# A fused attention and expert kernel on one core: the third and fourth score tile of a step wait together, and three edits in the order behind the attention

## The chip, the cores and the metric

One NeuronCore of a Trainium2 chip runs the whole program. The metric is the device time of one execution in microseconds (us). Engines are named as in the profile: PE is TensorE's matmuls, PEld its weight loads, ACT is ScalarE, DVE is VectorE, POOL is GpSimd, SP is the queue that issues most DMAs. L944 is line 944 of the kernel before.

## The reference

A text stream x (4 sequences, 512 tokens, 256 wide) attends to a context of 1601 rows, and then goes through a mixture of experts:

```python
x = x + tanh(g_xattn[0]) * xattn(layernorm(x), ctx, ...)     # 16 heads of 16
x = x + tanh(g_ffn[0])   * experts(layernorm(x), ...)        # one shared, 8 routed, top 2

def xattn(x, y):
    q, k, v = x @ Wq + bq, y @ Wk + bk, y @ Wv + bv
    out = softmax(q k^T / 4) v                                # per head
    return relu(out @ W1 + b1) @ W2 + b2
```

All is float32. In most products a float32 operand is split into a rounded part ("hi") and a rest ("lo"), both of which TensorE takes in one pass; the product is then hi·hi + lo·hi + hi·lo.

## The kernel before, in words

The attention runs in 16 units (a batch of the four, times a group of four heads). A unit has 13 steps, one for each tile of up to 128 context rows, so there are 208 steps. The engines have queues of their own, written out by hand, and semaphores between them.

A step m on PE has, in this order: two score tiles (`st`, L944: 64 contraction rows, 128 context rows by 512 tokens), a "score pair" (`score`, L929, which computes scores of the next unit of which only maxima are wanted), the other jobs of the step (Q, K, V, W1, ... in other units few or none), a second score pair, two more score tiles, and the values of the step before (`pv`, L959: four heads side by side in 32 columns each, read from `probs`). ACT turns each score tile into exponentials (`exp`, L770, which writes `probs`), DVE takes the maxima of the score pairs (L1079).

Score tiles and jobs share a ring of three PSUM banks (`ring_ps`). Whoever takes a bank waits in `free_bank` until the bank's user before it has been read. The tiles of a step are 4m-1, 4m, 4m+1 and 4m+2; in a step without jobs the third (4m+1) takes the bank of tile 4m-2, and the fourth (4m+2) that of tile 4m-1. So the fourth waits for the exponential of the first tile of its own step. Tiles of an even number use rows 0 to 63 of the array, those of an odd number rows 64 to 127 (`rows` in `st`), so each pair of a step has one of each. In the last unit the ring has five banks, two of them from `gu_ps`.

Behind the steps stand the last jobs: SUM (transposes the result), OT (transposes it back, split by ACT into `ot_hi` and by DVE into `ot_lo`), four W1 products of six matmuls each, two W2 products. Between them `begin_shared(t, f, k)` starts the shared expert for token tiles 0 and 1: half k of the contraction of gate (f=0) or up (f=1) into `gu_ps`. The last step also has the job LG (transposes of logits, L892), which reads what DVE copied from the job LT (L887, L1098). After a barrier (L370) the second part of the kernel runs; its first matmuls are `gate_up(1)` (L1463), then the transposes of tile 0's hidden values (L1472).

Of the kernel before, what the change touches and what calls it, by code (L numbers as in the profile page):

```python
# [28 lines left out]
B, N, D = 4, 512, 256  # L29
# [10 lines left out]
MT = (M + P - 1) // P  # L40
# [3 lines left out]
UNITS = B * H // 4  # L44
# [264 lines left out]
def attention(nc, I, x1, stats, mv, veps, power, rstd, tg, ident, rows_dram,  # L309
# [16 lines left out]
    def tiles_of(m):  # L326

        first, last = (2 if m > MT * (UNITS - 1) else 0), (2 if m >= MT * (UNITS - 1) else 0)
        return list(range(max(4 * m - 1 + first, 0), min(4 * m + 3 + last, 4 * MT * UNITS)))
# [40 lines left out]
    with ExitStack() as ctx:  # L370
# [418 lines left out]
        def _(pe):  # L789
# [29 lines left out]
            def do(job):  # L819
# [39 lines left out]
                elif kind == "V":  # L859
                    _, b, g = job  # L860
                    for mt in range(2 * g, min(2 * g + 2, MT)):
                        last = value_tile(slot, b, mt)
                elif kind == "MX":
                    pe.wait_ge(mx_ready, job[1] + 1)
                    last = nc.tensor.transpose(slot[0:16, 0:P], mx[:].rearrange("p h t -> p (h t)"), ident[:])
                elif kind == "SUM":
                    pe.wait_ge(pv_free, job[1] + 2)
                    for t in range(NT):
                        last = nc.tensor.transpose(slot[:, t * P:(t + 1) * P], osb[:, t * P:(t + 1) * P], ident[:])
                elif kind == "OT":  # L870
                    _, b, dt = job
                    pe.wait_ge(free_dve, freed["SUM", 4 * b + 3])
                    heads = slice(dt * P // HD, (dt + 1) * P // HD)
                    for t in range(NT):
                        last = nc.tensor.transpose(slot[:, t * P:(t + 1) * P],
                                                   onT[:, t, heads, :].rearrange("p h d -> p (h d)"), ident[:])
                elif kind == "XT2":
                    _, b, k = job
                    pe.wait_ge(xn2_ready, NT * (b + 1))
                    for t in range(NT):  # L880
                        last = nc.tensor.transpose(slot[:, t * P:(t + 1) * P],
                                                   xn2[:, b * NT + t, k * P:(k + 1) * P], ident[:])
                elif kind == "LT":
                    b = job[1]
                    pe.wait_ge(free_dve, freed["XT2", b, 1])
                    for k in range(2):
                        last = nc.tensor.matmul(slot[0:E, :], wr[:, k, :], xn2T[:, b * NT:(b + 1) * NT, k, :],  # L887
                                                start=(k == 0), stop=(k == 1))
                elif kind == "LG":
                    pe.wait_ge(free_dve, freed["LT", job[1]])  # L890
                    for t in range(NT):
                        last = nc.tensor.transpose(slot[:, t * E:(t + 1) * E], across[:, t * P:(t + 1) * P],  # L892
                                                   ident[0:E, 0:E])
                elif kind == "W1":
                    _, b, f = job
                    pe.wait_ge(w1_parted, 2 * min(b + 1, B - 1))
                    pe.wait_ge(free_dve, freed["OT", b, 1])
                    products = [(w, x) for k in range(2) for w, x in ((w1_hi[:, k], ot_hi[:, k, :]),
                                                                      (w1_lo[:, k], ot_hi[:, k, :]),
                                                                      (w1_hi[:, k], ot_lo[:, k, :]))]  # L900
                    for n, (w, x) in enumerate(products):
                        last = nc.tensor.matmul(slot, w[:, f * P:(f + 1) * P], x, start=(n == 0),
                                                stop=(n == len(products) - 1))
                elif kind == "W2":
                    _, b, half = job
                    pe.wait_ge(free_act, freed["W1", b, F1 // P - 1])
                    for i in range(2):
                        t = 2 * half + i
                        for k in range(F1 // P):
                            last = nc.tensor.matmul(slot[:, i * D:(i + 1) * D], h1[:, k, t * P:(t + 1) * P],  # L910
                                                    w2[:, k, :], start=(k == 0), stop=(k == F1 // P - 1))
# [56 lines left out]
            for item in first + early:  # L968
# [4 lines left out]
                else:  # L973
                    do(item)
            pe.wait_ge(free_dve, freed["MX", 0])
            for u, mt, chunk, jobs in steps:
                m = MT * u + mt
                lead = 2 if m > 0 else 1
                for idx in tiles_of(m)[:lead]:
                    st(idx)  # L980
                for pair in chunk[0:1]:
                    score(pair)
                for job in jobs:
                    if not ahead_of_values(u, job):
                        do(job)
                for pair in chunk[1:2]:
                    score(pair)
                for idx in tiles_of(m)[lead:]:
                    st(idx)
                for pair in chunk[2:]:  # L990
                    score(pair)
                for job in jobs:
                    if ahead_of_values(u, job):
                        do(job)
                if m > 0:
                    pv(m - 1)
            pv(MT * UNITS - 1)

            def begin_shared(t, f, k):
# [5 lines left out]

            pe.wait_ge(ws_loaded, 80)
            pe.wait_ge(free_dve, freed["XT2", 0, 1])
            waits = [("SUM", UNITS - 1), ("OT", B - 1, 0), ("W1", B - 1, 0), ("W2", B - 1, 0)]
            for job in last_jobs:
                if job in waits:  # L1010
                    n = waits.index(job)
                    begin_shared(0, n // 2, n % 2)
                do(job)
            pe.wait_ge(exp_done, 4 * MT * UNITS)
            begin_shared(1, 0, 0)

        @block.vector
        def _(dve):
# [163 lines left out]
def experts(nc, I, O, x1, stats, mv, veps, power, rstd, tg, ident, rows_dram, picked_dram, shared, lists,  # L1182
            gate_hi, up_hi, gu_ps, gu_full):
    xn2, xn2T, wgu_s, wd_s, wr, rb, logit = shared
    with ExitStack() as ctx:
# [195 lines left out]
        def _(pe):  # L1381
# [50 lines left out]
            def gate_up(i):  # L1432
# [9 lines left out]
                for f in range(2):  # L1442
# [6 lines left out]
                            pe.wait_ge(owner_ready, 1)  # L1449
                        owners[r + 1] = pe.value_load(owner[0:1, r + 1:r + 2], min_val=0, max_val=E - 1)  # L1450
                    if tile_of(i) is not None:
                        begun = i == 1 and f == 0
                        products = [(xn2T[:, tile_of(i), k, :], wgu_s[:, k, f * F2:(f + 1) * F2])
                                    for k in range(begun, 2)]
                    else:
                        e, begun = bass.ds(owners[r], 1), False
                        products = []
                        for k in range(2):
                            hi, lo = (up_hi if f else gate_hi)[:, e, k, :], wgu_lo[:, e, k, f * F2:(f + 1) * F2]
                            x_hi, x_lo = xb_hi[:, r % 2, k, :], xb_lo[:, r % 2, k, :]  # L1460
                            products += [(x_hi, hi), (x_hi, lo), (x_lo, hi)]
                    for n, (x, w) in enumerate(products):
                        last = nc.tensor.matmul(gu_ps[:, i % 2, f, :], x, w, start=(n == 0 and not begun),  # L1463
                                                stop=(n == len(products) - 1))
                last.then_inc(gu_full, 1)

# [295 lines left out]
```

## Time and profile before

| | |
|---|---|
| median of 3 runs | 1035.18 us (1034.99 to 1036.46) |
| the profiled execution | 1034.86 us |
| its span, first to last instruction | 1033.1 us |
| granted clock of TensorE | 0.998 |
| PE busy | 1011.9 us, 98% |
| DVE busy | 680.7 us, 66% |
| ACT busy | 612.1 us, 59% |

The steps of the attention lie between about 56 and 714 us of the span, the last jobs between 714 and 734 us. PE counts as busy nearly everywhere, since a matmul's record lasts until its last result is out; how close the array is to its limit must be read from the starts of the matmuls.

### The profile page before, as it was taken

How to read it: one execution, taken by the hardware profiler on the slowest of the kernel's cores; microseconds unless marked ns; L12 is line 12 of the kernel's file. 1: busy time of each engine (PE TensorE's matmuls, PEld its weight loads, DVE VectorE, ACT ScalarE, POOL GpSimd, SP SyncE). 2: the span in 40 equal slices, each digit the busy share in tenths (PEclk: the TensorE clock that was granted, in tenths of full speed). 3: DMA queues.
4: the chain of work that ended last, by engine and by line, in shares of the span. 5: the costliest groups of instructions: out<-in, count | busy, mean ns of one | idle time of the engine just before them, and what ended most of it. 6: DMA issues, size and time to landing. Idle time of an engine off the chain costs nothing. (4 is left out here: it accounts for less than half of the span.)

```text
span 1033.1 us, 15853 instructions
## 1 busy us (share of the span) xinstructions
PE 1011.9 (98%) x5821; PEld 559.6 (54%) x5821; DVE 680.7 (66%) x929; ACT 612.1 (59%) x1144; POOL 227.8 (22%) x225
## 2 busy tenths in 40 slices
PE   8899999999999999999999999998999999999998
PEld 5434445434445434544544453333666888888865
DVE  4999886896787798588788768712487322222227
ACT  3167777886677777577787767774375222222211
POOL 6129300105400103610010031020002333333310
PEclk9999999999999999999999999999999999999999
DMA  9263030430302403203033030011591111111107
GB/s 220 72 169 63 2 64 4 125 64 2 64 14 52 107 22 64 55 10 65 1 64 65 1 64 1 18 66 41 175 336 30 39 51 53 53 51 52 48 26 244
DMA packets 38282, 70.17 MB, mean 68 GB/s; under 512 B 6848, under 2 KB 23360, under 8 KB 38208
## 3 DMA queue, kind: packets, MB, share of 16 engines
q1 hardware_dynamic: 33072, 57.88, 21.6%
q0 software_dynamic: 3744, 10.23, 3.2%
q10 hardware_dynamic: 1392, 1.05, 0.4%
q8 instruction: 49, 0.80, 0.3%
q14 instruction: 25, 0.20, 0.1%
HBM read 33.70 MB, written 9.31 MB: 42 GB/s over the span
## 5 line engine op out<-in xcount | busy, mean ns | idle before, releaser
L770 ACT ACTIVATE probs<-ring_ps 128x512 f32<-128x512 f32 x816 | 434.0, 598 | 125.8 <-PE ring_ps L944 118.8
L1079 DVE TENSOR_REDUCE mpart<-gu_ps 128x2 f32<-128x1024 f32 x384 | 456.4, 1220 | 71.3 <-PE gu_ps L929 71.2
L944 PE MATMUL ring_ps<-qst,kst 64*128 64x512 f32 x816 | 221.8, 459 | 3.0 <-ACT probs L770 2.1
L959 PE MATMUL pv_ps<-probs,vp 128*32 128x512 f32 (+2 forms) x1664 | 222.7, 604 | 0.6 <-ACT osb L701 0.6
L944 PEld LDWEIGHTS ring_ps<-qst,kst 64*128 64x128 f32 x816 | 97.3, 180 | 205.4 <-ACT probs L770 116.2
L929 PE MATMUL gu_ps<-kst,qst 63*128 63x512 f32 (+1 forms) x1024 | 179.7, 396 | 8.7 <-DVE mpart L1079 7.5
L929 PEld LDWEIGHTS gu_ps<-kst,qst 63*128 63x128 f32 x1024 | 91.7, 185 | 64.1 <-DVE mpart L1079 40.3
L1309 ACT ACTIVATE h_sb<-gu_ps 128x512 f32<-128x512 f32 x55 | 32.8, 596 | 133.6 <-PE gu_ps L1463 133.6
L1516 DVE TENSOR_TENSOR h_sb<-h_sb,gu_ps 128x512 f32<-128x512 f32 x55 | 37.7, 686 | 112.6 <-ACT h_sb L1309 112.1
L1483 PE MATMUL y_ps<-wd,hT 128*128 x312 | 73.8, 379 | 0.0
L1300 POOL DMA_INDIRECT picked<-ysb,target x39 | 38.5, 988 | 131.5 <-DVE ysb L1557 131.5
L959 PEld LDWEIGHTS pv_ps<-probs,vp 128*32 128x32 f32 (+2 forms) x1664 | 32.9, 107 | 57.8 <-issue 42.4
L1463 PE MATMUL gu_ps<-wgu_lo,xb_hi 128*128 x156 | 61.2, 392 | 0.0
L304 POOL TENSOR_SCALAR veps<-mv 128x4 f32<-128x4 f32 x8 | 1.9, 233 | 266.9 <-DVE mv L1048 113.9
L1483 PEld LDWEIGHTS y_ps<-wd,hT 128*128 128x128 f32 x312 | 56.2, 190 | 6.0
L630 POOL TENSOR_SCALAR c_hi<-w 128x1024 fp32r<-128x1024 f32 x3 | 8.3, 2775 | 223.2 <-PE ring_ps L806 223.2
L1463 PE MATMUL gu_ps<-cold,parts 128*128 128x512 f32 x118 | 53.8, 597 | 0.3 <-PEq L370 0.3
L1287 POOL DMA_INDIRECT xb<-rows,token x39 | 40.7, 1044 | 56.7 <-DVE token L1635 34.8
L1315 ACT ACTIVATE xb_hi<-t_ps 128x256 fp32r<-128x256 f32 x39 | 15.0, 385 | 49.3 <-PE t_ps L1429 49.3
L1557 DVE COPY ysb<-y_ps 128x256 f32<-128x256 f32 x39 | 16.6, 425 | 33.1 <-PE y_ps L1483 33.1
L742 ACT ACTIVATE vp<-ring_ps 128x512 f32<-128x512 f32 (+1 forms) x28 | 15.9, 568 | 32.2 <-PE ring_ps L806 32.2
L1463 PEld LDWEIGHTS gu_ps<-cold,parts 128*128 128x128 f32 x118 | 22.4, 193 | 22.7 <-issue 21.9
(240 smaller groups left out, 1251.8 us busy)
## 6 DMA issues: line engine op xcount, KB each, us to landing
kst<-parts SPq DMA_DIRECT2D x45, 401.0 KB, 5.3
qst<-parts SPq DMA_DIRECT2D x48, 128.0 KB, 4.5
wgu<-in_WgT SPq DMA_DIRECT2D x16, 256.0 KB, 8.2
wgu<-in_WuT SPq DMA_DIRECT2D x16, 256.0 KB, 8.3
wd<-in_WdT SPq DMA_DIRECT2D x8, 512.0 KB, 9.8
wgu<-picked SPq DMA_DIRECT2D x8, 512.0 KB, 7.4
cold<-in_ctxT SPq DMA_DIRECT2D x3, 800.5 KB, 4.2
cold<-in_ctxT SPq DMA_DIRECT2D x6, 400.2 KB, 5.9
```

Of the source, the lines that this page charges most:

```text
L770: nc.scalar.activation(probs[0:w, m % NPB, h, :], bank_of(("st", idx))[0:w], ACT.Exp, scale=SCALE).then_inc(exp_done, 1)
L929: last = nc.tensor.matmul(out, qst[u % NKB][rows, p, i * P:(i + 1) * P], kst[u % NKB][rows, p, keys], start=True, stop=True)
L944: nc.tensor.matmul(bank_of(("st", idx))[0:w], kst[u % NKB][rows, h // 2, mt * P:mt * P + w], qst[u % NKB][rows, h // 2, :], start=True, st ...
L959: last = nc.tensor.matmul(pv_ps[32 * h:32 * h + c1 - c0, :], values[:, c0:c1], probs[0:w, m % NPB, h, :], start=(mt == 0), stop=(mt == MT ...
L1079: nc.vector.tensor_reduce(mpart[:, :, p, t, q], s_ps[:, n % NSP], AX.X, ALU.max).then_inc(s_free, 1)
L1287: pool.indirect_dma_start(xb[:, r % NXB, :], None, rows_dram[:], bass.IndirectOffsetOnAxis(ap=token[:, r:r + 1], axis=0)).then_inc(xb_load ...
L1300: pool.indirect_dma_start(picked_dram[:], bass.IndirectOffsetOnAxis(ap=target[:, r:r + 1], axis=0), ysb[:, r % NXB, :], None).then_inc(y_s ...
L1309: nc.scalar.activation(h_sb[:, i % 2, :], gu_ps[:, i % 2, 0, :], ACT.Silu).then_inc(silu_done, 1)
L1463: last = nc.tensor.matmul(gu_ps[:, i % 2, f, :], x, w, start=(n == 0 and not begun), stop=(n == len(products) - 1))
L1483: last = nc.tensor.matmul(y_of(i), hT[:, i % 2, k, :], w, start=(k == 0), stop=(k == FK - 1))
L1516: nc.vector.tensor_tensor(h_sb[:, i % 2, :], h_sb[:, i % 2, :], gu_ps[:, i % 2, 1, :], ALU.mult).then_inc(h_ready, 1)
L1557: nc.vector.tensor_copy(ysb[:, r % NXB, :], y_ps[:, 0:D]).then_inc(y_out, 1)
```

## The change

- In the steps of all units but the last, PE waits for the banks of the third and the fourth tile before it issues the third.
- The last step's LG moves from ahead of the values of step 206 to behind them.
- W1: the four products with `ot_hi` go first and wait for ACT's part alone; the wait for DVE's `ot_lo` stands before the fifth.
- `begin_shared`: the second half of the up product goes ahead of W1 with the first, half a gate of tile 1 goes ahead of W2, and the other half stands at the end. The second part's `gate_up(1)` then has no gate matmuls.

```diff
@@ W1 in do(job)
-                    pe.wait_ge(free_dve, freed["OT", b, 1])
-                    products = [(w, x) for k in range(2) for w, x in ((w1_hi[:, k], ot_hi[:, k, :]),
-                                                                      (w1_lo[:, k], ot_hi[:, k, :]),
-                                                                      (w1_hi[:, k], ot_lo[:, k, :]))]
+                    pe.wait_ge(hi_ready, hi_count["OT", b, 1])
+                    products = ([(w[:, k], ot_hi[:, k, :]) for k in range(2) for w in (w1_hi, w1_lo)] +
+                                [(w1_hi[:, k], ot_lo[:, k, :]) for k in range(2)])
                     for n, (w, x) in enumerate(products):
+                        if n == 4:
+                            pe.wait_ge(free_dve, freed["OT", b, 1])
@@ the steps
+            last_logits = steps[-1][3][-1]
...
+                if u < UNITS - 1:
+                    for idx in tiles_of(m)[lead:]:
+                        free_bank(bank_owner(("st", idx)))
                 for idx in tiles_of(m)[lead:]:
                     st(idx)
...
-                    if ahead_of_values(u, job):
+                    if ahead_of_values(u, job) and job != last_logits:
                         do(job)
                 if m > 0:
                     pv(m - 1)
+            do(last_logits)
             pv(MT * UNITS - 1)
@@ behind the steps
-            waits = [("SUM", UNITS - 1), ("OT", B - 1, 0), ("W1", B - 1, 0), ("W2", B - 1, 0)]
+            pe.wait_ge(exp_done, 4 * MT * UNITS)
             for job in last_jobs:
-                if job in waits:
-                    n = waits.index(job)
-                    begin_shared(0, n // 2, n % 2)
+                if job == ("SUM", UNITS - 1):
+                    begin_shared(0, 0, 0)
+                elif job == ("OT", B - 1, 0):
+                    begin_shared(0, 0, 1)
+                elif job == ("W1", B - 1, 0):
+                    begin_shared(0, 1, 0)
+                    begin_shared(0, 1, 1)
+                elif job == ("W2", B - 1, 0):
+                    begin_shared(1, 0, 0)
                 do(job)
-            pe.wait_ge(exp_done, 4 * MT * UNITS)
-            begin_shared(1, 0, 0)
+            begin_shared(1, 0, 1)
@@ gate_up(i) of the second part
-                                    for k in range(begun, 2)]
+                                    for k in range(2) if (i, f) != (1, 0)]
```

PE's queue in a step whose third tile takes the bank of a job, before: two tiles, two score pairs, the third tile, the fourth tile, the values.

```order
L944 MATMUL ring_ps<-qst0,kst0 128x512 [waits exp_done] x2
L929 MATMUL gu_ps<-kst2,qst2 128x512 [waits s_free]
L929 MATMUL gu_ps<-kst2,qst2 128x512
L929 MATMUL gu_ps<-kst2,qst2 128x512 [waits s_free]
L929 MATMUL gu_ps<-kst2,qst2 128x512
L944 MATMUL ring_ps<-qst0,kst0 128x512 [waits free_dve]
L944 MATMUL ring_ps<-qst0,kst0 128x512 [waits exp_done]
L959 MATMUL pv_ps<-probs,vp 32x512 [waits exp_done]
```

The same place of the changed kernel, from the second score pair on.

```order
L930 MATMUL gu_ps<-kst2,qst2 128x512 [waits s_free]
L930 MATMUL gu_ps<-kst2,qst2 128x512
L945 MATMUL ring_ps<-qst0,kst0 128x512 [waits free_dve,exp_done]
L945 MATMUL ring_ps<-qst0,kst0 128x512 [waits exp_done]
L960 MATMUL pv_ps<-probs,vp 32x512 [waits exp_done]
```

The matmuls stand where they stood; the wait of the fourth tile now stands ahead of the third as well. In a step without jobs both waits are for `exp_done`, so that the row reads as before ("[waits exp_done] x2"), but there too a semaphore instruction with both counts has come in front. PE's queue has 366 semaphore instructions before and 561 after: 195 more, one for each step of 15 units.

PE's queue at the end of the steps and behind it, before: LT, LG, values of step 206, values of step 207, then the last jobs up to the first W1.

```order
L887 MATMUL gu_ps<-parts,wr 8x512
L892 MATMUL ring_ps<-ident,across 128x8 [waits free_dve]
L892 MATMUL ring_ps<-ident,across 128x8 x3
L959 MATMUL pv_ps<-probs,vp 32x512 [waits exp_done]
L959 MATMUL pv_ps<-probs,vp 32x512 x2
L959 MATMUL pv_ps<-probs,vp 17x512
L959 MATMUL pv_ps<-probs,vp 32x512 [waits exp_done]
```

The same place after.

```order
L887 MATMUL gu_ps<-parts,wr 8x512
L960 MATMUL pv_ps<-probs,vp 32x512 [waits exp_done]
L960 MATMUL pv_ps<-probs,vp 32x512 x2
L960 MATMUL pv_ps<-probs,vp 17x512
L892 MATMUL ring_ps<-ident,across 128x8 [waits free_dve]
L892 MATMUL ring_ps<-ident,across 128x8 x3
L960 MATMUL pv_ps<-probs,vp 32x512 [waits exp_done]
```

LG has moved behind the values of step 206 and ahead of those of step 207. The third place is the first W1 of the last jobs; after the change PE has there:

```order
L1007 MATMUL gu_ps<-cold,parts 128x512 x2
L903 MATMUL ring_ps<-ot_hi,c0_hi 128x512 [waits hi_ready,w1_parted,free_dve]
L903 MATMUL ring_ps<-ot_hi,c1_both 128x512
L903 MATMUL ring_ps<-ot_hi,c0_hi 128x512
L903 MATMUL ring_ps<-ot_hi,c1_both 128x512
L903 MATMUL ring_ps<-xt_hi,c0_hi 128x512 [waits free_dve]
```

Before, one `begin_shared` matmul (L1001) stood there instead of two, and W1's first matmul waited for `free_dve` and `w1_parted`. (`xt_hi` is the memory of `ot_lo`, `c0_hi` and `c1_both` that of W1's parts.)

## Rows read from the trace of the kernel before

**Rows 1.** The page: engine totals, and the group of exponentials.

```profile
PE 1011.9 (98%) x5821; PEld 559.6 (54%) x5821; DVE 680.7 (66%) x929; ACT 612.1 (59%) x1144; POOL 227.8 (22%) x225
...
L770 ACT ACTIVATE probs<-ring_ps 128x512 f32<-128x512 f32 x816 | 434.0, 598 | 125.8 <-PE ring_ps L944 118.8
```

**Rows 2.** Busy time (PE, PEld, DVE, ACT, POOL) in a unit without jobs.

```profile
181.00:214.00 33.00, 33.00 (x220) 13.20 (x216) 28.72 (x30) 26.20 (x52) 3.71 (x2) 1.00 0.36 98
```

**Rows 3.** Timeline of one step without jobs: start, length, [idle before <-releaser].

```profile
210.31 0.18 PEld L944 LDWEIGHTS ring_ps<-qst,kst 64*128 64x128 f32 x2 [0.84 <-ACT probs L770]
210.84 2.07 ACT L770 ACTIVATE probs<-ring_ps 128x512 f32<-128x512 f32 x4 [0.80 <-PE ring_ps L944]
211.11 0.88 PE L944 MATMUL ring_ps<-qst,kst 64*128 64x512 f32 x2
211.49 0.18 PEld L944 LDWEIGHTS ring_ps<-qst,kst 64*128 64x128 f32 x1 [0.40 <-ACT probs L770]
211.92 1.06 PE L959 MATMUL pv_ps<-probs,vp 128*32 128x512 f32 x8
212.90 0.18 PEld L944 LDWEIGHTS ring_ps<-qst,kst 64*128 64x128 f32 x2 [0.84 <-ACT probs L770]
```

**Rows 4.** Waits of PEld (us, times, longest) in 60:93, 181:214, 215:256, 307:350, 639:672.

```profile
PEld ring_ps L944 <- ACT probs L770: 10.2, 15, 0.8
...
PEld ring_ps L944 <- ACT probs L770: 12.3, 20, 0.8
...
PEld ring_ps L944 <- ACT probs L770: 6.0, 9, 0.8
...
PEld ring_ps L944 <- ACT probs L770: 2.1, 3, 0.8
...
PEld ring_ps L944 <- ACT probs L770: 14.0, 21, 0.9
```

**Rows 5.** Timeline at SUM and OT, whose waits stand in semaphore instructions.

```profile
714.28 0.60 ACT L701 ACTIVATE osb<-pv_ps 128x512 f32<-128x512 f32 x1 [3.65 <-PE pv_ps L959]
715.00 0.14 PEld L869 LDWEIGHTS ring_ps<-ident,osb 128*128 128x128 f32 x1 [0.56 <-issue]
...
716.03 0.42 DVE L1144 TENSOR_TENSOR onT<-ring_ps,rden 128x256 f32<-128x256 f32 x1
716.57 0.14 PEld L875 LDWEIGHTS ring_ps<-ident,onT 128*128 128x128 f32 x1 [0.84 <-issue]
```

**Rows 6.** Timeline of a step with a V job: third and fourth tile, values.

```profile
158.71 0.40 PE L944 MATMUL ring_ps<-qst,kst 64*128 64x512 f32 x2
...
159.04 1.07 PE L959 MATMUL pv_ps<-probs,vp 128*32 128x512 f32 x8
```

**Rows 7.** Timeline of the last step: LT, its copy, LG, values.

```profile
709.23 1.88 PE L887 MATMUL gu_ps<-parts,wr 128*8 128x512 f32 x4 [0.18 <-ACT probs L770]
...
711.15 0.68 DVE L1098 COPY across<-gu_ps 8x512 f32<-8x512 f32 x1 [2.96 <-PE gu_ps L887]
...
711.98 0.38 PE L892 MATMUL ring_ps<-ident,across 8*128 8x8 f32 x4 [0.86 <-DVE across L1098]
...
712.29 1.92 PE L959 MATMUL pv_ps<-probs,vp 128*32 128x512 f32 x16
```

**Rows 8.** Timeline at the first W1 of the last jobs.

```profile
717.50 1.02 PE L1001 MATMUL gu_ps<-cold,parts 128*128 128x512 f32 x2
...
718.78 0.74 DVE L1115 SCALAR_TENSOR_TENSOR xt_hi<-ring_ps,bv,ot_hi 128x512 fp32r<-128x512 f32 x1
...
719.67 0.47 PE L902 MATMUL ring_ps<-ot_hi,c_hi 128*128 128x512 f32 x1 [1.15 <-DVE xt_hi L1115]
```

**Rows 9.** Timeline at the start of the second part.

```profile
734.69 2.81 PE L1463 MATMUL gu_ps<-cold,parts 128*128 128x512 f32 x6 [0.30 <-PEq L370]
...
736.58 0.69 DVE L1516 TENSOR_TENSOR h_sb<-h_sb,gu_ps 128x512 f32<-128x512 f32 x1
...
737.32 0.42 PEld L1472 LDWEIGHTS ht_ps<-ident,h_sb 128*128 128x128 f32 x4 [0.64 <-DVE h_sb L1516]
```

More of the change, by code:

```diff
@@ L1451, in gate_up @@
                     if tile_of(i) is not None:
-                        begun = i == 1 and f == 0
                         products = [(xn2T[:, tile_of(i), k, :], wgu_s[:, k, f * F2:(f + 1) * F2])
-                                    for k in range(begun, 2)]
+                                    for k in range(2) if (i, f) != (1, 0)]
                     else:
-                        e, begun = bass.ds(owners[r], 1), False
+                        e = bass.ds(owners[r], 1)
                         products = []
@@ L1462, in gate_up @@
                     for n, (x, w) in enumerate(products):
-                        last = nc.tensor.matmul(gu_ps[:, i % 2, f, :], x, w, start=(n == 0 and not begun),
+                        last = nc.tensor.matmul(gu_ps[:, i % 2, f, :], x, w, start=(n == 0),
                                                 stop=(n == len(products) - 1))
```

## The prediction

> **What bounds the kernel now.** I read the page first: PE is busy 98% of the span, ACT 59%, DVE 66% [rows 1]. That does not tell which of them a step waits for, so I went to the stretches and then to one step. A unit without jobs (181 to 214 us) has 13 steps in about 34 us, and DVE is busy 28.7 of 33 us and ACT 26.2 [rows 2]: neither is full. The timeline of one step shows why it takes 2.59 us all the same (210.31 to 212.90) [rows 3]. The reader is to follow one chain through it: the first pair of tiles starts at 210.31; its first exponential at 210.84, and it lasts 0.60 [rows 1], to 211.44; the fourth tile, whose bank that exponential frees, loads at 211.49, after an idle 0.40 that ACT ended; the values follow at 211.92, and the next step's first pair at 212.90. 0.53 + 0.60 + 0.05 + 0.43 + 0.98 = 2.59: the chain is closed, with no slack in it, and it runs through the wait of the fourth tile.
>
> How often is that so? The waits of the weight loads of L944 for ACT mix two kinds: the pair behind the values, 0.84 each (the values themselves lie in that time), and the fourth tile, 0.40 to 0.43. In 181 to 214 us there are 20 with 12.3 us: 9 of 0.84 and 11 of 0.43. In the same way 60 to 93 us has 6 of the short kind, 639 to 672 us has 9, 215 to 256 us has 4, and 307 to 350 us, a unit with many jobs, has 1 [rows 4]. The units repeat this by batch. Three units are like the first of these (11 each), units 13 and 14 have 9 each, unit 0 has 6, three units 4 each, six units 1 or 2: 33 + 18 + 6 + 12 + 9 = 78. Some of these waits are put down to the values or to another engine in the views, so I take 85 of the 195 changed steps as steps in which the fourth tile's wait closes the chain.
>
> **The joint wait.** It takes no matmul away. What it can do is start the third tile later, or change how PE waits.
>
> The third tile: in the step shown it started at 211.11, ran with nothing behind it, and the fourth came at 211.49 (the two records together 0.88) [rows 3]. They use different rows of the array, and the values stand behind the fourth. So delaying the third by 0.4 frees nothing, and nothing on PE is later for it. On ACT the third tile's exponential comes later: it followed the first two at 211.82 (four of them take 2.07 and one 0.60, so they start 0.49 apart) [rows 1, 3], and now needs the tile, 0.53 behind its start. With the tile at 211.56 it starts at 212.09 and ends at 212.69; its bank is wanted at 212.90. It is covered by 0.2 us. Without that cover it costs what it is late, up to 0.3 us a step; I put 0.5 us for the few steps with less room (ends of units, job steps).
>
> How PE waits: before, the fourth tile's own load carried the wait, and it started 0.05 us after the exponential's end (211.44 to 211.49) [rows 3]. Now the last wait to end stands in a semaphore instruction. The trace shows what that costs where it is already so: the exponential's place is taken by ACT's copy, which ends at 714.88, and SUM's load starts at 715.00, after 0.11 to 0.12; DVE's product ends at 716.45 and OT's load starts at 716.57, the same again [rows 5]. So the wait takes 0.115 instead of 0.05, 0.065 us more, on a chain without slack. In 85 steps that is 5.5 us. Below, it is nothing (if the engine hides it); above, it is 195 x 0.065 = 12.7 us (if every step passes it on). I take 5.5, since in the job steps the tiles come long after the exponentials and the matmuls of the jobs cover the instruction.
>
> The Trainium skill (Perfetto Trace Analysis, Identifying Dependency Chains) says that an instruction that waits for several engines may have semaphore instructions put in front of it; it gives no price. The rows above are the price, and the trace agrees that they stand there.
>
> **LG behind the values.** Before, PE stood from the end of LT until DVE's copy ended at 711.83, started LG at 711.98 and the values of 206 at 712.29, those of 207 one half of 1.92, some 0.88, later, at 713.17 [rows 7]. LT's fourth matmul record ends at 711.11; values can follow there at about 711.05 (0.07 before the end of the last record, as at 211.92 in [rows 3], where the tile before ran to 211.99). They take 0.98 until other work may start (211.92 to 212.90 [rows 3]), so LG starts at 712.03 and is past DVE's copy, and the values of 207 start 0.31 later, at 712.34. Gain: 0.83 us. If LG waited once more, the gain would be smaller, not below 0.
>
> **W1 and the begun products.** W1's first matmul stood at 719.67, 0.15 behind DVE's `ot_lo` (718.78 + 0.74 = 719.52). The begun product ahead of it started at 717.50 and has two records of 0.43 each, so four end at 719.22 [rows 8]. ACT's `ot_hi` is done before that. W1 starts at about 719.25: gain 0.42 us. Its fifth matmul comes 0.9 later and finds `ot_lo` done. The half gate ahead of W2 takes the place of the half up there, and the last one that of the one before: 0. W1 in the other three batches stands a step or more behind OT, so its new wait is long over: 0.
>
> In the second part `gate_up(1)` has four matmul records instead of six, 0.86 us less on PE. But the transposes behind it waited for DVE: 736.58 + 0.69 = 737.27, and their load starts at 737.32 [rows 9]. DVE's work there starts at the barrier and does not change. So 0; if the transposes had followed PE alone, 0.86.
>
> **Sum**, against the profiled execution: 1034.86 + 5.5 + 0.5 - 0.83 - 0.42 = 1039.6; it lies 0.3 below the median of the runs, so I say 1040.0 us. A difference under 0.2%, 2.1 us, is about what a measurement of this kernel cannot tell from no change.
>
> **Rivals.** (A) The semaphore instruction costs nothing in the steps, or DVE absorbs it: DVE is busy 28.7 of 33 us [rows 2], and a score pair that waits for it takes up what PE is late. For it: in units with jobs this must happen. Against it: in the step shown PE's wait for the fourth tile comes after both score pairs. Only the last jobs' 1.25 us remain, and the time is 1034.0 us.
>
> (B) Two tiles that start together leave the array sooner. In the job step the pair was together at 158.71 and the values came 0.33 later [rows 6]; behind the lone fourth tile they came 0.43 later [rows 3]. If the joint start earns that 0.10, it pays 0.10 - 0.065 = 0.035 in 85 steps, 3.0 us: 1034.9 + 0.3 - 3.0 - 1.25 = 1030.9 us. It decides as soon as it earns more than the 0.065 in these steps. Against it: at 158.71 the two had their weights loaded ahead, since nothing was waited for (records of 0.40 against 0.49), and a joint wait leaves both loads behind the wait. The Trainium skill (TensorE: Matmul & The Clock Gate, Part 3) has matmuls in different row groups run at once, which would speak for such a gain. The trace agrees on the overlap, but the chain here does not stand on the array's time.
>
> (C) The two counts in one semaphore instruction cost twice: 0.13 in 85 steps, 11 us, 1045 us. I see no row for it.
>
> **Numbers.** My forecast (1037.3 to 1042.5 alone) 0.62, A 0.19, B 0.14, C 0.05. Of A, most lies within 0.2% (1033.1 to 1037.3), a small part below it; a tenth of my own case, with half of the steps absorbed, lies there as well. Slower 0.62, same 0.22, faster 0.16. The range from 1032.0 to 1043.0 leaves out most of B and C.
>
> **What the profile will show.** In a step without jobs, third and fourth tile start together, 0.12 behind the first exponential's end, and the step takes 2.65 instead of 2.59 us; the unit from 181 us is 0.8 longer; units with many jobs are as long as before. The values of 206 start ahead of LG, W1 starts 1.75 behind the first begun product, and the last jobs, from the values of 207 to the barrier, are 0.4 shorter. PE is idle about 0.9 ahead of the second part's first transposes. I am wrong if the load of the third tile starts 0.05 behind the exponential, or if the values then come 0.33 behind the pair.

## The result and the profile after

The changed kernel takes 1039.7 us, the median of 6 runs (1038.48 to 1040.11), against 1035.17 us of the kernel before (6 runs, 1034.94 to 1036.46). The ratio is 1.0041, with a 95% interval of 1.0029 to 1.0054: it is slower, and the forecast of 1040.0 us is met. The profiled execution took 1039.84 us with a span of 1038.1 us, 5.0 us more than the span before, at a granted clock of 1.0. Below it turns out that two of the forecast's terms were off and that a third, of which it knew nothing, made up for them by luck.

The page, engine totals and exponentials (as in [rows 1]):

```profile
PE 1000.1 (96%) x5821; PEld 547.0 (53%) x5821; DVE 680.9 (66%) x929; ACT 621.6 (60%) x1144; POOL 230.1 (22%) x225
...
L770 ACT ACTIVATE probs<-ring_ps 128x512 f32<-128x512 f32 x816 | 442.5, 595 | 122.1 <-PE ring_ps L945 104.0
```

PE's busy time has gone down by 11.8 us while the kernel became slower: the records of two matmuls that start together lie over each other, and that time counts once. The number says nothing about the work; the starts do.

The timeline of one step without jobs, as in [rows 3] (L945 is now the score tile, L960 the values):

```profile
211.70 0.19 PEld L945 LDWEIGHTS ring_ps<-qst,kst 64*128 64x128 f32 x2 [0.84 <-ACT probs L770]
...
212.23 1.09 ACT L770 ACTIVATE probs<-ring_ps 128x512 f32<-128x512 f32 x2 [0.58 <-PE ring_ps L945]
...
212.90 0.22 PEld L945 LDWEIGHTS ring_ps<-qst,kst 64*128 64x128 f32 x2 [0.60 <-DVE mneg L1147]
212.93 0.50 PE L945 MATMUL ring_ps<-qst,kst 64*128 64x512 f32 x2 [0.25 <-issue]
213.36 0.15 PEld L960 LDWEIGHTS pv_ps<-probs,vp 128*32 128x32 f32 x8 [0.25 <-ACT probs L770]
...
214.35 0.18 PEld L945 LDWEIGHTS ring_ps<-qst,kst 64*128 64x128 f32 x2 [0.84 <-ACT probs L770]
```

The step takes 214.35 - 211.70 = 2.65 us, where it took 2.59. The first exponential ends 0.60 after 212.23, at 212.83; the third tile's load follows at 212.90, 0.07 behind it, and the fourth's 0.03 behind that. (The view names DVE as the releaser of 212.90, since the third tile of this step takes a bank that DVE has read, but it is ACT's exponential that ended just before.) The fourth tile's matmul stands 0.10 behind the exponential instead of 0.05, and the values again 0.42 behind it. The whole chain is the old one with some 0.05 us put in at one place.

The waits of PEld in 182 to 215 us, as in [rows 4]: there were 20 with 12.3 us, and the ones of the fourth tile are now of the third, which waits longer.

```profile
PEld ring_ps L945 <- ACT probs L770: 14.0, 21, 0.8
PEld pv_ps L960 <- ACT probs L770: 2.4, 10, 0.2
PEld gu_ps L930 <- DVE mpart L1090: 1.9, 7, 0.3
```

The last step, as in [rows 7]. The values of step 206 now follow LT at 715.42, LG stands at 716.85 and the values of 207 at 717.16:

```profile
715.42 1.42 PE L960 MATMUL pv_ps<-probs,vp 128*32 128x512 f32 x5
...
716.02 0.68 DVE L1109 COPY across<-gu_ps 8x512 f32<-8x512 f32 x1 [2.96 <-PE gu_ps L887]
...
716.85 0.38 PE L892 MATMUL ring_ps<-ident,across 8*128 8x8 f32 x4
...
717.16 1.06 PE L960 MATMUL pv_ps<-probs,vp 65*32 65x512 f32 x8
```

LG still starts 0.15 behind the end of DVE's copy (716.70), and no longer holds anything up: the values of 206 fill that time.

The first W1 of the last jobs, as in [rows 8], and the start of the second part, as in [rows 9]:

```profile
721.51 1.88 PE L1007 MATMUL gu_ps<-cold,parts 128*128 128x512 f32 x4
...
722.12 1.41 DVE L1126 SCALAR_TENSOR_TENSOR xt_hi<-ring_ps,bv,ot_hi 128x512 fp32r<-128x512 f32 x2 [1.66 <-ACT ot_hi L749]
...
722.83 0.80 PE L903 MATMUL ring_ps<-ot_hi,c_hi 128*128 128x512 f32 x1
...
738.22 1.96 PE L1473 MATMUL gu_ps<-cold,parts 128*128 128x512 f32 x4 [0.30 <-PEq L370]
...
740.10 0.69 DVE L1526 TENSOR_TENSOR h_sb<-h_sb,gu_ps 128x512 f32<-128x512 f32 x1
...
740.84 0.42 PEld L1482 LDWEIGHTS ht_ps<-ident,h_sb 128*128 128x128 f32 x4 [1.50 <-DVE h_sb L1526]
```

PEld idles 1.50 us ahead of the transposes, 0.86 more than before: the two matmuls that the second part no longer has are turned into idle time.

Where the 5.0 us of span went, by the starts of the same work in both traces:

| stretch | before | after | change |
|---|---|---|---|
| start of the last LT matmul | 710.52 | 715.39 | +4.87 |
| from there to the first begun product | 3.62 | 2.76 | -0.86 |
| from there to the first W2 of the last jobs | 12.25 | 11.76 | -0.49 |
| from there to the second part's first transposes | 10.95 | 10.93 | -0.02 |
| from there to the last output transfer's issue | 293.69 | 293.71 | +0.02 |
| from its issue to its landing | 1.69 | 3.15 | +1.46 |

The last line was in nobody's sum. Between 1034.5 and 1037.5 us the DMA view of the kernel after has the lines below: one packet on q8, which moves code, and one output transfer that takes 3.1 us to land. The kernel before has no line of q8 in its last 4 us, and its last two transfers have a median of 1.7 us.

```profile
q8 instruction: 1, 0.02, 3.0%
issues: line engine op xcount, KB each, median us to landing
out<-x SPq DMA_DIRECT2D x1, 128.0 KB, 3.1
```

### The profile page after: what moved, and what is told of

The parts are those of the page before. It is cut to its first block and busy times, and to the rows that moved or that the text cites. A ratio compares the mean times of both kernels' runs of the same rounds, so it can differ in the third digit from the quotient of the medians.

```text
span 1038.1 us, 16048 instructions
## 1 busy us (share of the span) xinstructions
PE 1000.1 (96%) x5821; PEld 547.0 (53%) x5821; DVE 680.9 (66%) x929; ACT 621.6 (60%) x1144; POOL 230.1 (22%) x225
## 5 line engine op out<-in xcount | busy, mean ns | idle before, releaser
L770 ACT ACTIVATE probs<-ring_ps 128x512 f32<-128x512 f32 x816 | 442.5, 595 | 122.1 <-PE ring_ps L945 104.0
L960 PE MATMUL pv_ps<-probs,vp 128*32 128x512 f32 (+2 forms) x1664 | 223.7, 604 | 0.6 <-ACT osb L701 0.6
L945 PE MATMUL ring_ps<-qst,kst 64*128 64x512 f32 x816 | 198.5, 469 | 18.0 <-ACT probs L770 14.7
L945 PEld LDWEIGHTS ring_ps<-qst,kst 64*128 64x128 f32 x816 | 80.2, 180 | 224.4 <-ACT probs L770 135.4
L930 PE MATMUL gu_ps<-kst,qst 63*128 63x512 f32 (+1 forms) x1024 | 177.1, 396 | 8.2 <-DVE mpart L1090 6.4
L960 PEld LDWEIGHTS pv_ps<-probs,vp 128*32 128x32 f32 (+2 forms) x1664 | 33.1, 107 | 57.3 <-issue 32.8
L1298 POOL DMA_INDIRECT xb<-rows,token x39 | 42.9, 1101 | 54.1 <-DVE token L1645 34.8
L1482 PEld LDWEIGHTS ht_ps<-ident,h_sb 128*128 128x128 f32 x220 | 27.2, 141 | 15.1 <-issue 5.8
```

What stands on the lines that cost most here:

```text
L770: nc.scalar.activation(probs[0:w, m % NPB, h, :], bank_of(("st", idx))[0:w], ACT.Exp, scale=SCALE).then_inc(exp_done, 1)
L930: last = nc.tensor.matmul(out, qst[u % NKB][rows, p, i * P:(i + 1) * P], kst[u % NKB][rows, p, keys], start=True, stop=True)
L945: nc.tensor.matmul(bank_of(("st", idx))[0:w], kst[u % NKB][rows, h // 2, mt * P:mt * P + w], qst[u % NKB][rows, h // 2, :], start=True, st ...
L960: last = nc.tensor.matmul(pv_ps[32 * h:32 * h + c1 - c0, :], values[:, c0:c1], probs[0:w, m % NPB, h, :], start=(mt == 0), stop=(mt == MT ...
L1298: pool.indirect_dma_start(xb[:, r % NXB, :], None, rows_dram[:], bass.IndirectOffsetOnAxis(ap=token[:, r:r + 1], axis=0)).then_inc(xb_load ...
L1482: last = nc.tensor.transpose(ht_ps[:, i % 2, k * P:(k + 1) * P], h_sb[:, i % 2, k * P:(k + 1) * P], ident[:])
```

## The experiments

Each kernel was run beside the kernel before, whose medians were 1035.09 us beside the first four, 1035.22 beside the next four and 1035.27 beside the last two. Ratios are to the kernel before, with their 95% intervals. "Closed steps" are the 124 of the 195 changed steps in which, in the trace of before, the fourth tile's load starts within 0.06 us of an exponential's end.

**What the joint wait and the other three edits do apart.** The changed kernel without the joint wait, which leaves the steps as they were:

```diff
-                if u < UNITS - 1:
-                    for idx in tiles_of(m)[lead:]:
-                        free_bank(bank_owner(("st", idx)))
                 for idx in tiles_of(m)[lead:]:
                     st(idx)
```

> The changed kernel without the joint wait: LG behind the values, W1 and the begun products alone. Its trace showed 0.86 us gained at LG and 0.49 us at W1, and 0 in the second part. If these are independent of the steps, the kernel is 1.35 us faster than before, 1033.8 us, and the steps take as long as before. Rival: the last output's transfer, which took 3.15 us in the changed kernel against 1.69 before, is slow because of the tail edits; then 1035.3 us, and the last transfer again takes about 3.1 us.

And the kernel before with those three lines put in and nothing else:

> The kernel before with the joint wait alone. The steps lose the 4.9 us that the changed kernel's trace shows up to the last step: 1040.1 us. If the slow last transfer (1.46 us) comes from the 195 added instructions through a code fetch that falls on it, the exact place of the fetch decides: up to 1041.5 us with it. Rival: the loss needs the other edits too; then below 1039 us.

Without the joint wait: 1033.87 us (11 runs), ratio 0.9992 (0.9982 to 1.0001). With it alone: 1040.01 us (5 runs), ratio 1.0046 (1.0032 to 1.0059). The two expectations hold: the whole loss is the joint wait's, and the other edits bring some 1.2 us that it buries. Its step, in the timeline of the kernel with the joint wait alone:

```profile
211.34 0.50 PE L944 MATMUL ring_ps<-qst,kst 64*128 64x512 f32 x2
...
212.54 0.22 PEld L944 LDWEIGHTS ring_ps<-qst,kst 64*128 64x128 f32 x2 [0.60 <-DVE mneg L1139]
...
213.99 0.50 PE L944 MATMUL ring_ps<-qst,kst 64*128 64x512 f32 x2
```

It is the step of the kernel after, 2.65 us.

**Is it the common start or the semaphore instruction?** Both edits here are made to the changed kernel without the joint wait. In the first both tiles start together, but the third tile's own matmul carries the later count and the fourth asks for nothing, so there is no semaphore instruction (where a job held one of the banks, the tiles wait as before):

```diff
@@ st
-                free_bank(bank_owner(("st", idx)))
+                if bank_freed_by is None:
+                    free_bank(bank_owner(("st", idx)))
+                elif bank_freed_by[0] == "later":
+                    pe.wait_ge(exp_done, bank_freed_by[1])
@@ the steps
-                for idx in tiles_of(m)[lead:]:
-                    st(idx)
+                rest = tiles_of(m)[lead:]
+                holders = [bank_owner(("st", idx)) for idx in rest]
+                if u < UNITS - 1 and len(rest) == 2 and all(h is not None and h[0] == "st" for h in holders):
+                    st(rest[0], ("later", max(h[1] for h in holders) + 1))
+                    st(rest[1], ("held",))
+                else:
+                    for idx in rest:
+                        st(idx)
```

> The tail edits, and a joint start without a semaphore instruction: where both banks were held by score tiles, the third tile's own load waits for the later exponential and the fourth's has no wait; where a job held one of them, the tiles wait as before. Theory from the changed kernel's trace (third load 0.069 behind the exponential, fourth 0.101, against 0.051 for the fourth before): 0.032 of the 0.050 lost per step is the second load of the pair being issued behind the wait, so here the fourth load comes 0.083 behind, 88 steps lose 0.032 each, 2.8 us, and the kernel takes 1036.6 us. Rival: all the loss is the semaphore instruction; the fourth load comes 0.054 behind, nothing is lost, 1033.9 us. Second rival, a pair that starts together clears the array sooner: below 1033 us.

In the second the tiles start as before, apart, and the fourth tile alone has its wait in a semaphore instruction:

```diff
-                for idx in tiles_of(m)[lead:]:
+                for n, idx in enumerate(tiles_of(m)[lead:]):
+                    if n == 1 and u < UNITS - 1:
+                        free_bank(bank_owner(("st", idx)))
                     st(idx)
```

> The tail edits, and in the same 195 steps a semaphore instruction with the fourth tile's wait ahead of the fourth alone; the third starts early, as before. Theory: the semaphore instruction itself costs 0.018 (0.069 against 0.051), so 88 steps lose 1.6 us: 1035.4 us, and up to 1.5 more if the code fetch falls on the last transfer. Rival of my prediction: the instruction costs 0.065 as at SUM and OT, 5.7 us: 1039.5 us. Rival: it costs the whole 0.050 and the pair's common start nothing: 1038.2 us.

The first took 1035.04 us (11 runs, ratio 1.0002, 0.9993 to 1.0011), with loads 0.051 and 0.054 us behind the exponential: the 0.03 us between the two loads, which I had put down to the common start, are not there without the instruction. The other took 1041.25 us (5 runs, ratio 1.0056, 1.0043 to 1.007), with the fourth tile's load 0.113 behind. Both expectations had the size wrong, in opposite directions, and together they say that the semaphore instruction is the cause of nearly all of the loss: the common start without it costs the closed steps 0.35 us in all. (The first kernel's median is 1.17 us above that of the kernel without the joint wait, 1033.87; its runs lie at 1034.07 to 1035.38 and four of them at 1036.72 to 1037.09, and its trace shows no more than the 0.35.) A step of the kernel with the instruction ahead of the fourth tile:

```profile
213.01 1.58 ACT L770 ACTIVATE probs<-ring_ps 128x512 f32<-128x512 f32 x3 [0.81 <-PE ring_ps L945]
213.07 0.18 PEld L945 LDWEIGHTS ring_ps<-qst,kst 64*128 64x128 f32 x1
...
213.72 0.18 PEld L945 LDWEIGHTS ring_ps<-qst,kst 64*128 64x128 f32 x1 [0.46 <-ACT probs L770]
```

The exponential ends at 213.61 and the load stands at 213.72; before it was 0.05 behind. (Its profiled execution, 1043.13 us, also lost 1.36 us once in the last unit, where the edit does nothing.)

**Does an instruction cost anything whose count is there already?** Where several counts are asked for, the matmul carries the one asked for first and the instruction the others. So the order of two waits decides which of them stands in the instruction. In the changed kernel the later count does, beside the older one that the matmul carries too; here the order is turned round:

```diff
-                    for idx in tiles_of(m)[lead:]:
+                    for idx in reversed(tiles_of(m)[lead:]):
                         free_bank(bank_owner(("st", idx)))
```

> The changed kernel with the two early waits asked in the other order (fourth tile's bank first). There are as many semaphore instructions as in the changed kernel, but the instruction now holds only the count of the third tile's bank, which has long been reached, and the third tile's matmul itself carries the later count, of the first exponential. Theory (only the wait that ends last costs something when it stands in a semaphore instruction): the loads of the third and the fourth tile come 0.05 us behind the exponential as in the tail-only kernel, steps of 2.60 us, time 1034.0 to 1034.5, or 1035.5 if the code transfer falls on the last output transfer again (1.45 us). Rival (every semaphore instruction costs PE's queue its time, wherever the wait is): as slow as the changed kernel, 1038.3 to 1039.7.

And 195 instructions that never wait, ahead of the values, on top of the last jobs' edits:

```diff
                 pe.wait_ge(exp_done, 4 * (m + 1))
+                if u < UNITS - 1:
+                    pe.wait_ge(pool_ready, 2)
```

> The tail edits alone, plus a semaphore instruction ahead of each step's values in 15 units (195 of them), whose count (POOL's at the start of the kernel) has been reached since the start. Theory (an instruction whose count is there costs the steps nothing, since the values' own wait, 0.4 us behind the fourth tile, covers it; what it does is lengthen the program, so that a 16 KB piece of code is fetched on top of the last output transfer): steps 2.60 us, last transfer 3.1 instead of 1.7 us, 1035.3. Rival 1 (each costs 0.02 to 0.06 on the closed chain, between the fourth tile and the values): 1036 to 1041. Rival 2 (the long last transfer of the changed kernel and of the fourth-tile kernel has another cause than the program's length): 1033.9.

1034.83 us (11 runs, ratio 0.9993, 0.9984 to 1.0002) and 1034.59 us (11 runs, ratio 0.9994, 0.9985 to 1.0004). Both have the 561 semaphore instructions of the changed kernel and hardly any of its loss. The 124 closed steps together are longer by 0.38 and 0.13 us, against 4.61 in the changed kernel. The step of the kernel with the order turned round, with a common start and 2.60 us:

```profile
210.64 0.50 PE L945 MATMUL ring_ps<-qst,kst 64*128 64x512 f32 x2
211.18 2.26 ACT L770 ACTIVATE probs<-ring_ps 128x512 f32<-128x512 f32 x4 [0.60 <-PE ring_ps L945]
211.82 0.19 PEld L945 LDWEIGHTS ring_ps<-qst,kst 64*128 64x128 f32 x2 [0.58 <-ACT probs L770]
...
213.24 0.49 PE L945 MATMUL ring_ps<-qst,kst 64*128 64x512 f32 x2
```

The exponential ends at 211.77 or 211.78, and the pair's loads stand at 211.82, 0.05 behind. The waits that the traces record in this step agree: here the third tile's load waits for ACT's count and the instruction for DVE's alone, while in the changed kernel the load waits for DVE's and the instruction for both. The theory holds, and its rival (each instruction costs its time) falls. The part of it on the program's length falls too: here the last transfer took 1.7 us.

**Why 0.05 a step in one case and 0.065 in the other?** First the number of counts, with two in the instruction ahead of the fourth tile:

```diff
                     if n == 1 and u < UNITS - 1:
                         free_bank(bank_owner(("st", idx)))
+                        free_bank(bank_owner(("st", idx - 1)))
```

> As the kernel with a semaphore instruction ahead of the fourth tile alone (1041.3 us, load 0.113 us behind the exponential, step +0.065), but the instruction holds two counts, the fourth tile's and the third's, as it does in the changed kernel. Theory (how late the load is depends on where the instruction stands and not on how many counts it holds): the fourth tile's load again 0.113 behind the exponential, 1041.3 less up to 0.5. Rival (an instruction with two counts is quicker after the last of them): load at 0.07, steps +0.02 to +0.03, 1037 to 1038.

It took 1040.29 us (5 runs, ratio 1.0049, 1.0036 to 1.0063), with the load again 0.113 behind the exponential and the closed steps longer by 6.13 us, as with one count (6.20). Not the number, then. Next what the matmul behind the instruction carries. In the changed kernel it is an old count, ahead of the fourth tile it was the fresh one. So once the changed kernel with the fresh count on the third tile's matmul, and once the other with the old one on the fourth's:

```diff
@@ the changed kernel
-                    for idx in tiles_of(m)[lead:]:
+                    for idx in 2 * tiles_of(m)[-1:]:
                         free_bank(bank_owner(("st", idx)))
@@ the instruction ahead of the fourth tile
-                        free_bank(bank_owner(("st", idx)))
+                        free_bank(bank_owner(("st", idx - 1)))
```

> The changed kernel with other counts in the same places: the semaphore instruction ahead of the third tile still holds both counts, but the third tile's own matmul now also carries the later one, which has only just been reached. In the changed kernel the matmul behind the instruction carries the older count and its load comes 0.069 us behind the exponential (steps +0.050); where the instruction stands ahead of the fourth tile its matmul carries the same count as the instruction, and the load comes 0.113 behind (steps +0.065). Theory (it is this second look at the same fresh count that makes the one dearer than the other): the third tile's load comes 0.11 behind here, the fourth's 0.03 later, and the steps lose 0.06 to 0.09, time 1041 to 1043. Rival (the place in the queue makes it): loads at 0.069 and 0.101 as in the changed kernel, 1038.5 to 1039.7.

> As the kernel with a semaphore instruction ahead of the fourth tile alone (load 0.113 us behind the exponential, steps +0.065, 1041.3 us), but the fourth tile's matmul now carries the third tile's older count and the instruction alone holds the fourth's. Theory of the second look: load at 0.069, steps +0.02, about 1036. Rival (the place in the queue makes it): load at 0.113, steps +0.065, 1040 to 1041.

1038.24 us (5 runs, ratio 1.0034, 1.0021 to 1.0047), loads at 0.069 and 0.101; and 1039.89 us (6 runs, ratio 1.0052, 1.0038 to 1.0067), load at 0.114. Both stayed as their place in the queue had them, so the theory behind these two runs (a second look at the same fresh count makes the load later) fell twice. The timeline of the second:

```profile
212.44 2.06 ACT L770 ACTIVATE probs<-ring_ps 128x512 f32<-128x512 f32 x4 [0.80 <-PE ring_ps L945]
212.50 0.18 PEld L945 LDWEIGHTS ring_ps<-qst,kst 64*128 64x128 f32 x1
...
213.15 0.18 PEld L945 LDWEIGHTS ring_ps<-qst,kst 64*128 64x128 f32 x1 [0.47 <-issue]
```

The traces also record the semaphore instructions themselves, and there the two places differ. First the one of the changed kernel's step at 212.9, then the one of the kernel with the instruction ahead of the fourth tile, at 213.7 (the three numbers are the shortest, median and longest record, in ns):

```profile
L798 PEldq EVENT_SEMAPHORE  x1: 589/589/589, 212.3 to 212.3; - x1
...
L794 PEldq EVENT_SEMAPHORE  x1: 51/51/51, 213.6 to 213.6; - x1
```

In the changed kernel, in the one with the joint wait alone and in the one with the fresh count on the third tile's matmul, the record begins 0.13 us or more ahead of the exponential's end in all 124 closed steps, ends 0.041 to 0.045 behind it, and the load starts 0.024 to 0.027 after that. In the three kernels with the instruction ahead of the fourth tile the record begins only 0.036 to 0.038 behind the exponential's end, lasts 0.051 (as does that of an instruction whose count is there already), and the load again starts 0.024 to 0.026 later. The instructions at SUM and OT in the kernel before, from which the forecast took its price, are of this second kind: 0.051 long, beginning about 0.04 behind the end of ACT's copy and of DVE's product. So it is dearer where the record begins only when the count comes. Why it begins no earlier there (the last matmul ahead of it is a lone third tile, and a score pair in the changed kernel) stays open.

The kernel with the fresh count on the third tile's matmul is also a second sample of the changed kernel: its steps are the same, its last transfer takes 1.7 us, and its median is 1.5 us lower. Its runs lie at 1037.95 to 1038.24 (three) and at 1039.63 and 1039.83, so the medians alone would be weak evidence.

**LG alone.** The kernel before with `do(last_logits)` behind the loop:

```diff
+            last_logits = steps[-1][3][-1]
...
-                    if ahead_of_values(u, job):
+                    if ahead_of_values(u, job) and job != last_logits:
                         do(job)
                 if m > 0:
                     pv(m - 1)
+            do(last_logits)
```

> The kernel before with LG moved behind the values of step 206 and nothing else. The two-trace comparison put 0.86 us on this move. Theory: the values of 207 and SUM come 0.86 earlier and nothing behind takes it back: 1034.2 to 1034.3 us, steps unchanged. Rival: the wait behind it (SUM's for ACT's copy, OT's for DVE) takes it back, 1035.1.

1034.21 us (11 runs, ratio 0.9989, 0.998 to 0.9998), as expected. In its timeline the copy, LG, the values of 207 and the first begun product, as in [rows 7]:

```profile
711.44 0.68 DVE L1100 COPY across<-gu_ps 8x512 f32<-8x512 f32 x1 [2.96 <-PE gu_ps L887]
...
712.26 0.38 PE L892 MATMUL ring_ps<-ident,across 8*128 8x8 f32 x4
...
712.58 1.06 PE L959 MATMUL pv_ps<-probs,vp 65*32 65x512 f32 x8
...
713.57 1.12 PE L1003 MATMUL gu_ps<-cold,parts 128*128 128x512 f32 x2
```

From the last LT matmul (710.81) to 713.57 it is 2.76 us, 0.86 less than before and the same as in the changed kernel. From 713.57 to the first W2 (725.84) it is 12.27, as before (12.25), so the 0.49 us there belong to W1 and the begun products: without the joint wait that stretch is 11.78.

## Why the prediction was right, and where it was off

**What bounds the kernel** was read rightly: the chain through the fourth tile's wait is closed, and what is put into it comes out of the step.

**The joint wait, 5.5 us: right mechanism, both factors off.** I took 85 steps by 0.065 us. There are 124 closed steps; 95 of them became longer by more than 0.03 us, by 0.049 on average, and make 4.63 us of it. The count was low, because the view of the waits lists the fourth tile's wait in 73 of the 124 only: in the other 51 PEld had been idle for less than 0.15 us before the load, and no idle time is listed there. The price was high: the instruction ahead of the third tile costs 0.05, and the 0.065, read from SUM and OT [rows 5], holds for one ahead of the fourth. The loads of the shown step stand 0.07 and 0.10 behind the exponential, not 0.12, and the unit from 181 us is 0.64 us longer, not 0.8. Of the 29 closed steps that did not become longer by more than 0.03 us (they changed by -0.045 to +0.030), 15 are those with the transposes of maxima (L865, one in a unit), and the timeline of after shows their cover. The transposes wait for the second exponential, which ends 0.5 behind the first:

```profile
210.03 0.22 PEld L945 LDWEIGHTS ring_ps<-qst,kst 64*128 64x128 f32 x2 [0.67 <-ACT probs L770]
210.06 0.50 PE L945 MATMUL ring_ps<-qst,kst 64*128 64x512 f32 x2 [0.26 <-ACT probs L770]
210.50 0.09 PEld L865 LDWEIGHTS ring_ps<-ident,mx 128*16 128x16 f32 x1 [0.26 <-ACT probs L770]
```

For the other 14 I did not follow it.

**The third tile's later start, 0.5 us**: 0.35 in the kernel with one wait and 0.38 in the one with the order turned round. A small cost, as said.

**Sum of the steps**: 6.0 forecast, 4.87 measured up to LT (0.22 of it ahead of the second step, where the other kernels scatter between -0.2 and +0.6).

**LG, -0.83**: -0.86, in the changed kernel and in that with LG's move alone. **W1 and the begun products, -0.42**: -0.49. W1's first matmul stands 1.32 behind the first begun product and not 1.75, but its record is 0.80 long and starts while the begun products still run (721.51 + 1.88 = 723.39), so only the stretch up to W2 tells the gain. **The second part, 0**: 0, with the two matmuls' 0.86 us seen as idle time.

**Not in the sum**: the last output transfer, +1.46 us in the profiled execution. 1034.86 + 4.87 - 0.86 - 0.49 + 1.46 = 1039.84, the profiled time. So the forecast of 1040.0 owes its closeness to luck: 1.1 us too much in the steps, 1.5 us missed at the end. The changed kernel's runs lie between 1039.48 and 1040.11 but for one at 1038.48, and the sum without the long transfer is 1038.4.

**The rivals.** A (nothing lost, 1034.0) is what happens when the instruction holds a count that is there: 1034.83 and 1034.59. As a forecast for this change it was wrong. DVE did not absorb it. B (a pair leaves the array sooner) fell: the values come 0.42 behind the pair, as they came behind the lone fourth tile. C (two counts cost twice) fell: two counts cost what one does (6.13 against 6.20 us).

The Trainium skill (Perfetto Trace Analysis, Identifying Dependency Chains) says that instructions waiting for several engines may have semaphore instructions put ahead of them. The trace agrees, and adds that two counts of one and the same semaphore, ACT's, are enough for it (the joint wait alone adds 4.9 us to the median).

## What to carry to other kernels

Of this change, take the last jobs' edits and leave the joint wait: 1033.87 us is the lowest median here, 1.2 us below the kernel before, which the interval (0.9982 to 1.0001) does not quite tell from no change.

## What the runs showed of the hardware that was not expected

A load whose own matmul carries the wait starts 0.05 us after the exponential's end. Behind a semaphore instruction that ends with the same exponential it starts 0.069 after it in one place of the queue (and the next tile's load 0.03 later instead of 0.003) and 0.113 in another, whatever the number of counts (tried in the second place) and whatever the matmul carries. In the first place the instruction's record begins before the count comes and ends 0.044 behind the exponential; in the second it begins only 0.037 behind it and is 0.051 long. In both the load starts 0.025 after the record's end.

The last output transfer (128 KB) took 3.1 us in two of the twelve profiled executions, those of the changed kernel and of the one with the instruction ahead of the fourth tile, and 1.7 us in the other ten. In these two a 16 KB transfer of code starts 0.56 us after its issue (1034.55 and 1035.11; 1037.92 and 1038.48), and in none of the ten does one fall on it. Three kernels with as many semaphore instructions as the changed one have their last code transfer about 1 us after the span's end, and three have it 2.8, 3.3 and 7.6 us ahead of the last output's issue, so their number does not decide it. In one of these, with the instruction ahead of the fourth tile and the old count on its matmul, the code transfer begins 0.17 us ahead of the issue of an earlier output, and that one takes 1.94 us; in another, one that begins 0.70 us ahead of an issue leaves it at 1.69. That the code transfer makes the output late is argued from this coincidence; no edit tested it.
